# First pieces of w1 and x loaded through ScalarE's DMA queue

## What is computed

```
attn   = (w1^T w2^T) * sparse_mask                     # 512 x 512, independent of x
layer1 = gelu(x attn + b2)
layer2 = where(query_sel & row_sel, x weight^T + bias, 0)
         query_sel, row_sel from softmax(10 * x centroids^T) > 0.01
layer3 = softmax(q k^T / sqrt(128)) v Wo + bo,  q, k, v = x Wqkv + bqkv
layer4 = layer2 once more, on the new x
```

## Time and profile before

| | us |
|---|---|
| median of 3 runs | 279.13 |
| lowest, highest | 278.44, 280.58 |
| profiled execution | 278.25 |
| its span | 276.5 |
| TensorE busy in the span | 268.4 |
| VectorE, ScalarE, GpSimd busy | 196.7, 176.8, 158.8 |

### The profile page before, as it was taken

The page is one execution under the profiler, slowest core; times in us unless marked ns, Lnnn a source line. Parts: engine busy times, 40 slices in busy tenths (PEclk is TensorE's granted clock), DMA queues, the critical chain, the costliest instruction groups (busy, mean ns, idle before and its releaser), DMA issues.

```text
span 276.5 us, 4419 instructions
## 1 busy us (share of the span) xinstructions
PE 268.4 (97%) x1392; PEld 224.2 (81%) x1392; DVE 196.7 (71%) x410; ACT 176.8 (64%) x358; POOL 158.8 (57%) x192
## 2 busy tenths in 40 slices
PE   7899999999999999999999999999999999999894
PEld 7787888888888888789988888888888888877673
DVE  3888988505926867775399796788259466867996
ACT  4855886465476785449899887777645576675400
POOL 4693988265495481289897994970730537113910
PEclk9999999999999999999999999999999999999998
DMA  6999064800000000000000000000000000000087
GB/s 230 356 370 344 12 207 177 303 0 0 2 0 0 2 0 2 2 0 0 2 0 0 4 1 0 2 0 0 2 2 0 0 2 1 0 2 0 13 306 288
DMA packets 10246, 18.23 MB, mean 66 GB/s; under 512 B 1200, under 2 KB 1968, under 8 KB 10224
## 3 DMA queue, kind: packets, MB, share of 16 engines
q1 hardware_dynamic: 10224, 17.96, 18.5%
HBM read 13.76 MB, written 4.19 MB: 65 GB/s over the span
## 4 chain that ended last, share of the span: by engine, by line
PE 88%; issue 4%; POOL 2%; DVE 2%; DMA 2%; ACT 1%; SPq 1%; DVEq 0%; POOLq 0%; ACTq 0%
PE m_bank L966 70%; PE t_bank L1059 11%; PE m_bank L1139 5%; DMA x_tok<-in_L_attn_a_x 2%; POOL y_tok L546 1%; PE t_bank L1065 1%; PE m_bank L1019 1%; DVE y_tok L925 1%; DVE x_tok L949 0%; ACT odd_hi L613 0%; POOL rstd L458 0%; SPq L384 0%; DVE y_tok L936 0%; SPq L387 0%; PE m_bank L1086 0%
## 5 line engine op out<-in xcount | busy, mean ns | idle before, releaser
L966 PE MATMUL m_bank<-ffn_hi,even_hi 128*128 128x512 f32 x96 | 39.0, 406 | 0.2 <-DVE y_tok L925 0.2
L966 PE MATMUL m_bank<-ffn_lo,even_hi 128*128 128x512 f32 x96 | 37.7, 392 | 0.0
L966 PE MATMUL m_bank<-ffn_hi,even_lo 128*128 128x512 f32 x96 | 37.4, 390 | 0.0
L546 POOL TENSOR_TENSOR y_tok<-y_tok,x_tok 128x512 f32<-128x512 f32 x16 | 20.4, 1296 | 25.4 <-ACT y_tok L719 25.4
L570 ACT ACTIVATE ones_and_squares<-x_tok,mv 128x512 bf16<-128x512 f32 x44 | 31.5, 717 | 4.1 <-DVE x_tok L872 3.7
L526 POOL TENSOR_TENSOR y_tok<-y_tok,bias_f 128x512 f32<-128x512 f32 x16 | 20.8, 1314 | 16.2 <-ACT y_tok L664 16.2
L454 POOL TENSOR_SCALAR ve<-mv 128x1 f32<-128x1 f32 (+1 forms) x20 | 5.3, 264 | 36.1 <-ACT ones_and_squares L570 35.0
L458 POOL TENSOR_TENSOR rstd<-ve,half 128x1 f32<-128x1 f32 (+1 forms) x31 | 23.9, 771 | 2.6
L775 DVE TENSOR_TENSOR even_lo<-t_bank,even_hi 128x512 fp32r<-128x512 f32 x24 | 16.2, 683 | 12.7 <-ACT even_hi L613 12.5
L775 DVE TENSOR_TENSOR odd_lo<-t_bank,odd_hi 128x512 fp32r<-128x512 f32 x28 | 18.8, 685 | 6.2 <-ACT odd_hi L613 6.0
L966 PE MATMUL m_bank<-odd_hi,wqkv_hi 128*128 128x512 f32 (+1 forms) x60 | 21.5, 358 | 0.0
(11 more groups left out here) (186 smaller groups left out, 775.2 us busy)
## 6 DMA issues: line engine op xcount, KB each, us to landing
out<-x_tok SPq DMA_DIRECT2D x15, 256.0 KB, 2.3
x_tok<-in_L_attn_a_x SPq DMA_DIRECT2D x3, 1024.0 KB, 8.2
xn_odd<-in_L_attn_a_xt SPq DMA_DIRECT2D x2, 1024.0 KB, 6.5
x_tok<-in_L_attn_a_x SPq DMA_DIRECT2D x4, 256.0 KB, 4.2
y_tok<-in_L_attn_a_w SPq DMA_DIRECT2D x4, 256.0 KB, 5.1
w_raw<-in_L_attn_a_w SPq DMA_DIRECT2D x4, 256.0 KB, 5.3
xt_other<-in_L_ffn_weight SPq DMA_DIRECT2D x4, 256.0 KB, 6.8
y_tok<-in_L_attn_a_sparse_mask SPq DMA_DIRECT2D x4, 256.0 KB, 7.3
```

The lines of the kernel that those rows point to most:

```text
L546: pool.tensor_tensor(y_tok[:, n, :], y_tok[:, n, :], x_tok[:, n, :], ALU.add).then_inc(done[kind], 1)
L966: ins = pe.matmul(bank, a, w, start=(first and n == 0), stop=(last and n == count - 1))
```

## The change

SyncE's list no longer begins with `load.x0.0 load.w1.0`; it begins with `load.w2.0`. ScalarE gets a list of two loads, which it issues ahead of all its other steps: first `w1.0`, then `x0.0`. The semaphores are the same, so those who wait for the pieces wait as they did.

```diff
 SP_ORDER = """
-load.x0.0 load.w1.0 load.w2.0 load.x0.1 load.x0.2 load.w1.1 load.x0.3 load.w2.1 load.w2.2 load.w1.2 load.w1.3
+load.w2.0 load.x0.1 load.x0.2 load.w1.1 load.x0.3 load.w2.1 load.w2.2 load.w1.2 load.w1.3 load.w2.3 load.ffn.1
...
+AQ_ORDER = "load.w1.0 load.x0.0"
...
+AQ_STEPS = steps_of(AQ_ORDER)
...
-        ld = {key: sem("ld_" + "_".join(str(k) for k in key)) for kind, key in SP_STEPS if kind == "load"}
+        ld = {key: sem("ld_" + "_".join(str(k) for k in key)) for kind, key in SP_STEPS + AQ_STEPS if kind == "load"}
...
         @block.scalar
         def _(act):
+            for _, (what, c) in AQ_STEPS:
+                if what == "w1":
+                    act.dma_start(w1_raw[:, c, :], w1_d[c * P:(c + 1) * P, :]).then_inc(ld[what, c], 16)
+                elif what == "w2":
+                    act.dma_start(w2_raw[:, c, :], w2t_d[c * P:(c + 1) * P, :]).then_inc(ld[what, c], 16)
+                else:
+                    act.dma_start(x_tok[:, c, :], x_d[0][c * P:(c + 1) * P, :]).then_inc(ld[what, c], 16)
+
             for kind, key in ACT_STEPS:
```

More of the change, by code:

```diff
@@ L128 @@
 SP_ORDER = """
-load.x0.0 load.w1.0 load.w2.0 load.x0.1 load.x0.2 load.w1.1 load.x0.3 load.w2.1 load.w2.2 load.w1.2 load.w1.3
[L130 to L133, removed]
+load.w2.0 load.x0.1 load.x0.2 load.w1.1 load.x0.3 load.w2.1 load.w2.2 load.w1.2 load.w1.3 load.w2.3 load.ffn.1
+load.ffn.0 load.cen load.ffn.2 load.sparse.0 load.ffn.3 load.sparse.1 load.sparse.2 load.sparse.3 load.small
+load.x.1 load.b2 load.xt.1 load.x.3 load.late load.x.2 load.bias load.xt.2 load.xt.3 store.2.3 store.1.0
+store.0.0 store.0.1 store.1.3 store.3.2 store.1.1 store.0.3 store.2.1 store.3.0 store.0.2 store.1.2 store.2.0
+store.3.1 store.2.2 storeh.3.3.0 storeh.3.3.1
 """
+AQ_ORDER = "load.w1.0 load.x0.0"
 def steps_of(text):
```

## The result

The changed kernel takes 280.61 us (median of 20 runs, 279.54 to 282.19); the kernel before, run beside it, 278.67 (278.23 to 280.58).

What follows compares the result with a forecast made beforehand. TensorE's fixed order of matrix products was taken as the bound, with almost only the head movable. A 1.1 us later attn.0.1 on the median of 279.13 gave 280.2 us, range 278.7 to 282.6.

Steps and rivals of the forecast that it cites:

- the step that decides: Loads at the head: x0.0 moves from first place to third or fourth, making attn.0.1 1.1 us late.
- the 1% bound: Whole kernel: about 1%, 2.8 us, is what a measurement can tell from no change; slower by more had chance 0.13.
- clock holds: Main case, chance 0.50: x0.0 lands third or fourth and TensorE's clock stays up; 280.2 us.
- T: Time at which VectorE first uses x0.0: 3.40 before, forecast 5.4, between 4.6 and 6.2.
- the 0.9 us around w2.0: Loading time lost near w2.0 before the change; left open whether due to that tensor, moment or queue place.
- third and fourth places: Landing places assumed for x0.0: 4.6 and 5.3 with the loss gone, 5.5 and 6.2 with it kept.
- The second path: From x0.0 through GpSimd, norm.1.0.0 on ScalarE and the transposes to attn.0.1: T + 4.3.
- VectorE's path: VectorE's in-order steps from the first statistic through w2lo.0: attn.0.1 can't start before T + 4.0.
- The third path: From stats.1.0.1 through norm.1.0.1 and w2lo.1 to attn.1: T + 6.2, a shift of T - 4.9, less than attn.0.1's.
- point of indifference: At the head, first use of x0.0 at 4.25; below it nothing is lost.
- The clock: Rival, chance 0.27: TensorE's clock falls in the 2.7 us gap after attn.0.0, adding 0.3 to 2.2; 281.5 us.
- The two issues: Loads added ahead on ScalarE: 0.42 and 0.38 us, up to twice that, hidden with 1.0 us to spare.

Runs made afterwards that it cites:

- e5: Changed kernel with x0.0 back at the head of SyncE's queue, so ScalarE issues only w1.0; 278.08 us, ratio to the kernel before 0.9977.
- e11: Changed kernel with x0.0 behind x0.2 on SyncE's queue, ScalarE issuing only w1.0, and 15 filling matmuls behind attn.0.0; 281.0 us, ratio to before 1.0075.
- e1: Kernel before, all loads still on SyncE's queue, but ordered w2.0, w1.0, x0.1, x0.0, x0.2; 282.69 us, ratio to before 1.0135.
- e10: Changed kernel with 10 filling matmuls behind attn.0.0, a repeat of e3; 280.51 us, ratio to the kernel before 1.0056.
- e7: Changed kernel's two queues with the landing order of before: SyncE has x0.0, w2.0, x0.2, ScalarE w1.0, x0.1; 277.87 us, ratio to before 0.9974.
- e8: Changed kernel with ScalarE issuing only w1.0 and SyncE x0.0, x0.1, w2.0, x0.2; 278.47 us, ratio to the kernel before 1.0002.
- e6: Changed kernel with ScalarE's two issues exchanged, x0.0 first and w1.0 second; 278.87 us, ratio to the kernel before 1.001.
- e4: Changed kernel with w1lo.0 ahead of stats.1.0.0 in VectorE's order; 280.54 us, ratio to the kernel before 1.0057.
- e9: Changed kernel run once more, unaltered, on another chip; 280.89 us, ratio to the kernel before 1.007.
- e2: Changed kernel with x0.0 moved behind x0.2 on SyncE's queue, ScalarE issuing only w1.0; 282.61 us, ratio to the kernel before 1.0132.
- e3: Changed kernel with 10 filling matmuls on a constant behind attn.0.0; 280.52 us, ratio to the kernel before 1.0057.
- e12: Kernel of e10 with w2lo.0 one place earlier in VectorE's order, ahead of stats.1.0.2; 280.60 us, ratio to the kernel before 1.0059.

## Why the prediction came out as it did

**Right: the sign, the size class and the step that decides.** Predicted 280.2, measured 280.61, within 278.7 to 282.6 and below the 1% bound. The deciding step was the place of x0.0, and e5 and e11 show it from both sides. That the two times are only 0.4 apart is in part luck. The forecast was 1.1 us slower than before, and 1.9 was measured; the base of 279.13, a median of three, was 0.46 above the 278.67 of the twenty. And the forecast was the case "clock holds", which the median execution isn't.

**T.** Taken as 5.4 between 4.6 and 6.2, measured 5.62. What I had left open, to whom the 0.9 us around w2.0 belong, e1 answers: to loading with one queue at that time, since with another order the low rate came back at another piece. With one queue it fell to 246 and 258 GB/s in one microsecond, with two never below 311 in the twelve traces (from 3 to 6 us). My third and fourth places at 5.3 with the loss gone missed how slowly two queues start: the first pair was used at 4.20 and not at 3.95.

**The chains behind T.** The second path, through GpSimd and the transposes, set attn.0.1, as forecast, and it was shorter: 3.92 us (5.62 to 9.54) and not 4.3. The transposes had stood at 7.25 behind the products of attn.0.0, though they could load at 7.03, and the 2.75 us to norm.1.0.0 were 2.64. VectorE's path was shorter too, 3.7 and not 4.0, since the rows it was summed from held waits. T came 0.2 late and the path was 0.4 short, so attn.0.1 at 9.54 instead of 9.7 is two errors that nearly cancel. The third path, GpSimd's to attn.1, I had called harmless; there a term was mis-sized. I took 2.46 us from stats.1.0.1 to norm.1.0.1 from a row in which GpSimd's power ran in 0.58; here it ran beside w2lo.0 and took 1.13. norm.1.0.1 started at 10.15, 3.13 after its statistic (7.02), and attn.1 at 12.27 in place of the predicted T + 6.2 = 11.8. The 11.1 it was compared with was wrong as well: it came from the view of the chain, and in the timeline attn.1 had started at 10.88, so that even without the delay this path asked for a shift of T - 4.7 and not T - 4.9. attn.0.1 had moved by 0.99; the end moved by 1.42 and not by 1.1.

The trace of the kernel before had the warning. GpSimd's first power there ran beside w1lo.0 (4.61 to 5.30), its second ahead of w2lo.0 (7.84):

```profile
4.82 0.93 POOL L458 TENSOR_TENSOR rstd<-ve,half 128x1 f32<-128x1 f32 x1
...
7.50 0.58 POOL L458 TENSOR_TENSOR rstd<-ve,half 128x1 f32<-128x1 f32 x1
```

The forecast's point of indifference, T = 4.25, isn't confirmed. Where the power is held up (e10, e11) nothing would be lost at 4.15; where it isn't (e5, e7), T = 4.15 and 4.25 give a gain of 0.4, and attn.0.1 follows T by 4.0 and 3.9, which puts the point near 4.6 as an estimate.

**The clock.** The likeliest case was "clock holds" with 0.50 against 0.27. In 12 of 20 executions it fell. The mechanism was right, the price nearly so (0.3 to 2.2 us, measured 1.0 and 2.4 over the first group), the chance was not: a gap of 2.7 us was forecast, 2.52 came, and with it the clock fell in some executions and held in others. Beside the longest idle gap of TensorE in the first 11 us of each trace, the executions with a mean clock under 0.995:

| | longest gap, us | low clock |
|---|---|---|
| the four runs with a filler | 0.32 to 0.70 | none of 24 |
| e7 | 0.61 | none of 12 |
| kernel before | 0.84 | none of 58 |
| e5 | 0.86 | none of 12 |
| e8 | 1.02 | 1 of 12 |
| e6 | 1.51 | 1 of 12 |
| e4 | 2.24 | 6 of 6 |
| changed kernel, with e9 | 2.52 and 2.56 | 17 of 27 |
| e2 | 3.02 | 6 of 6 |
| e1 | 3.61 | 4 of 4 |

The risk grows with the gap, but the gap isn't all: e4's is shorter than the changed kernel's and its clock fell each time. Why isn't known. The median execution of the changed kernel is one of the second group, at its lower end: 1.1 us for the head, as medians have it, and 0.9 for the clock make 280.61 out of 278.67.

**Nothing else moved.** The two issues took 0.41 and 0.45 us on ScalarE, the table load came behind them at 1.64 and was hidden, as costed; SyncE's earlier issues brought nothing to the end.

## What to carry to other kernels

When a load is moved to a second queue, its place among all loads counts and not its place in its own list: ask which in-order engine has its consumer at the head, and what is queued behind that. A few hundred nanoseconds gained on what TensorE needs first are worth nothing if TensorE's next step waits for something else, and the longer gap between the two puts its clock at risk, in the changed kernel in some executions only: look at the single times and their clocks, not just at the median. And a path that is called harmless by its length in one trace can be longer in the next, when another engine's instruction has moved beside it. The second queue was worth having (e7, 0.9974) once the order was kept.

## What was not expected of the hardware

Two queues loaded faster than one in the first microseconds, in every trace:

| | queues | loads issued by ScalarE | GB/s, 2 to 6 us |
|---|---|---|---|
| kernel before, e1 | one | 0 | 301, 291 |
| e2, e5, e8, e11 | two | 1 | 327 to 332 |
| changed kernel, e3, e4, e6, e7, e9, e10, e12 | two | 2 | 349 to 363 |

Issuing wasn't what held one queue back: in the kernel before, five pieces (1.3 MB) were issued by 3.0 us, and 0.63 MB had moved by 4.0. The Trainium skill ("DMA: Bandwidth & Descriptors", Issuing engines are not separate DMA queues) has it that a second issuing engine saves issue time alone; from 9 to 12 us the rates are the same here (402 and 400 GB/s with one queue, 376 to 402 with two), but in this stretch the measurement says otherwise. What holds one queue back there wasn't found.

GpSimd's instructions on 128x1 operands doubled beside VectorE's tensor_tensor: 0.58 to 1.13, 0.27 to 0.67. The Trainium skill ("SBUF — State Buffer", Who interferes with whom) says that a VectorE instruction with two inputs in SBUF and a GpSimd instruction that reads SBUF exclude each other; the trace agrees, and the statistics, with one input, didn't slow it (0.58 at 8.94 beside 8.34 to 9.03). Being side by side isn't enough, though; hundredths of a microsecond decide. In the changed kernel w2lo.0 started 0.03 after the power (8.65 and 8.62), and the power took 1.13; in e7 it started 0.05 after, and the power took 0.59:

```profile
7.25 0.59 POOL L462 TENSOR_TENSOR rstd<-ve,half 128x1 f32<-128x1 f32 x1
7.30 0.68 DVE L750 TENSOR_TENSOR w2t_lo<-w_raw,w2t_hi 128x512 fp32r<-128x512 f32 x1
```

In all seven traces in which w2lo.0 started 0.03 to 0.04 after this power (the changed kernel, e1, e2, e3, e9, e10, e11), the power took 1.13 or 1.14. Only one trace has the other case.
